# Attention layer of a four-layer GNN: rows kept turned, logits and coefficients laid out by edge in DRAM, products on GpSimd

## The reference

```python
h = relu(layernorm(x))
x1 = leaky(h, 0.01) @ W1.T + b1
h1 = (x1 @ Wg.T).reshape(N, 4, 32)
a_src = sum(h1 * att_src, axis=-1)
a_dst = sum(h1 * att_dst, axis=-1)
alpha = leaky(a_src[src] + a_dst[dst], 0.2)
coeff = softmax of alpha over the edges of one dst
out = segment_sum(h1[src] * coeff[:, :, None], dst)
out = leaky(out.reshape(N, 128) + bias_g, 0.01) @ W2.T + b2
x = x + out
```

## Time and profile before

| | |
|---|---|
| three runs | 3823.89, 3836.2 and 3827.94 us; median 3827.94 us |
| profiled execution, span | 3830.4 us (first to last instruction) |
| busy in the span | PE 1893.7, DVE 1993.0, ACT 992.0, POOL 2403.2 us |
| stage 3 | about 1281 to 1961 us |
| stage 4 | about 1961 to 2012 us |
| stage 5 | about 2012 to 2190 us |

### The profile page before, as it was taken

The page is one execution under the profiler, slowest core; times in us unless marked ns, Lnnn a source line. Parts: engine busy times, 40 slices in busy tenths (PEclk is TensorE's granted clock), DMA queues, the critical chain, the costliest instruction groups (busy, mean ns, idle before and its releaser), DMA issues. The chain is left out here.

```text
span 3830.4 us, 41092 instructions
## 1 busy us (share of the span) xinstructions
PE 1893.7 (49%) x8918; PEld 1513.8 (40%) x8918; DVE 1993.0 (52%) x6228; ACT 992.0 (26%) x2804; POOL 2403.2 (63%) x2088
## 2 busy tenths in 40 slices
PE   0000011158887467777655523247777773555553
PEld 0000010047676345555534412235555553545453
DVE  6964310058889534334458745543333334766664
ACT  0000010046561034334323334432222221221211
POOL 0867777768880455556500066548888886888887
PEclk9999985578899755555558855556666666776776
DMA  2999622246570122222207634446666664655555
GB/s 83 303 297 326 198 54 57 52 57 85 81 118 16 33 58 63 60 62 64 57 20 221 196 98 119 121 108 126 121 121 127 120 121 109 137 122 128 124 124 84
DMA packets 449554, 437.59 MB, mean 114 GB/s; under 512 B 77870, under 2 KB 359507, under 8 KB 449169
## 3 DMA queue, kind: packets, MB, share of 16 engines
q1 hardware_dynamic: 280404, 283.91, 23.7%
q0 software_dynamic: 128576, 119.75, 21.5%
q10 hardware_dynamic: 40512, 33.32, 3.7%
HBM read 262.12 MB, written 174.67 MB: 114 GB/s over the span
## 5 line engine op out<-in xcount | busy, mean ns | idle before, releaser
L1706 DVE TENSOR_TENSOR_SCAN work<-work,bank 128x512 f32<-128x512 f32 (+1 forms) x343 | 426.4, 1265 | 420.9 <-PE bank L842 272.2
L643 POOL DMA_INDIRECT work<-d,idx_run_d x196 | 191.2, 975 | 417.7 <-DVEq L286 294.7
L710 POOL DMA_INDIRECT big<-out_dram,idx_src_d x196 | 187.3, 956 | 308.7 <-DVE sc_d L1859 131.9
L657 POOL DMA_INDIRECT out_dram<-big,idx_add_s x196 | 310.0, 1582 | 83.5 <-issue 55.5
L657 POOL DMA_INDIRECT out_dram<-big,idx_add_d x196 | 314.0, 1602 | 77.2 <-issue 59.4
L657 POOL DMA_INDIRECT out_dram<-work,idx_add_s x196 | 315.9, 1612 | 70.9 <-issue 58.8
L1200 ACT ACTIVATE work<-work 128x128 f32<-128x128 f32 x784 | 318.3, 484 | 115.3 <-DVE work L1701 99.6
L842 PE MATMUL bank<-ident,work 128*128 128x128 f32 x588 | 143.8, 391 | 413.3 <-ACT work L1200 145.9
L842 PEld LDWEIGHTS bank<-ident,work 128*128 128x128 f32 x588 | 93.4, 195 | 456.1 <-issue 207.2
L643 POOL DMA_INDIRECT work<-rec_d,idx_e_s x196 | 216.7, 1106 | 80.6 <-issue 58.5
L643 POOL DMA_INDIRECT work<-he,idx_last_s x196 | 193.7, 988 | 87.2 <-issue 59.5
(11 more groups left out here) (340 smaller groups left out, 5508.1 us busy)
## 6 DMA issues: line engine op xcount, KB each, us to landing
out_dram<-big SPq DMA_DIRECT2D x71, 726.0 KB
big<-in_x_dram SPq DMA_DIRECT2D x71, 704.0 KB
work<-flags_src SPq DMA_DIRECT2D x98, 256.0 KB
work<-flags_dst SPq DMA_DIRECT2D x98, 256.0 KB
edge_w<-work SPq DMA_DIRECT2D x49, 512.0 KB
work<-edge_w ACTq DMA_DIRECT2D x49, 512.0 KB
gat_h<-work SPq DMA_DIRECT2D x49, 256.0 KB, 2.0
work<-gat_h SPq DMA_DIRECT2D x49, 256.0 KB, 4.2
```

What stands on the lines that cost most here:

```text
L643: g_.indirect_dma_start(to, None, table_ap, bass.IndirectOffsetOnAxis(ap=f[:, at_:at_ + 1], axis=0)).then_inc(of_rows(name).of(G), 16)
L657: g_.indirect_dma_start(table[:, :], bass.IndirectOffsetOnAxis(ap=of[:, at_:at_ + 1], axis=0), row, None, compute_op=ALU.add).then_inc(add ...
L710: g_.indirect_dma_start(to[:, t * ROW:(t + 1) * ROW], None, table, bass.IndirectOffsetOnAxis(ap=of[:, at_:at_ + 1], axis=0)).then_inc(rows ...
L1706: return V.tensor_tensor_scan(to, flag_r[G.place][rows, :], of, before if G.from_(1) else 0.0, ALU.mult, ALU.add)
```

## The change

Stage 3: PE projects the other way round, with the weights standing in the array and the turned rows streaming: one matmul of 512 columns for the rows and two of 512 columns for the logits of the four heads. The rows are stored turned (features by edges), and the bias is added by ACT in `keep`. The logits come out as 4 partitions of 512 edges, get their constant on DVE in one instruction, and go to DRAM (`gat_logits`). On ACT the copy of the turned rows (`rows_on`) is put one group later, ahead of `keep`.

Stage 4: the logits are loaded from DRAM in the softmax layout, the leaky step is done there, and the coefficients are stored to DRAM (`gat_coefficients`).

Stage 5: each group loads its coefficients as four transfers, one per head, each spread over 32 partitions; two are issued by SP and two by ACT. POOL multiplies rows by coefficients; there is no transpose; DVE scans the products from SBUF. The leaky step is one DVE instruction on the scan's result and on ACT's scaled copy.

```diff
+        def load_coefficients(eng, G, heads):
+            if G.from_(UNROLL):
+                eng.wait_ge(GATSUM["h"], G.g - (UNROLL - 1))
+            for h in heads:
...
+                eng.dma_start(co_r[G.place][C * h:C * h + C, :], part.partition_broadcast(C)).then_inc(h_in.of(G), 16)
...
@@ SP, stage 3 and stage 5
+            def store_logits(G):
+                sp.wait_ge(GAT["logits"], G.g + 1)
...
+                sp.dma_start(part, lg_r[G.slot][0:H, :]).then_inc(h_stored.of(G), 16)
...
                 sp.dma_start(in_r[G.place], at(h_dram, G, 512)).then_inc(h_in.of(G), 16)
+                load_coefficients(sp, G, (0, 1))
...
@@ POOL, stage 5
+            def products(G):
+                h_in.wait(pool, "GATSUM", G)
+                if G.from_(2):
+                    pool.wait_ge(GATSUM["chained"], G.g - 1)
+                g_.tensor_tensor(h_r[G.slot], in_r[G.place], co_r[G.place], ALU.mult).then_inc(GATSUM["h"], 1)
+            for_groups(pool, products)
...
@@ PE, stage 3
-                x_, b = hT8[G.slot], bank[4 + G.slot]
-                T.matmul(b[:, :], one[0:1, :], bF4[0:1, :], start=True, stop=False)
-                for t in range(GROUP):
-                    T.matmul(b[:, t * P:(t + 1) * P], x_[:, t * P:(t + 1) * P], wts["WF"][:, :],
-                             start=False, stop=t == GROUP - 1)
-                for t in range(GROUP):
-                    o = bank[6 + G.slot][:, t * H:(t + 1) * H]
-                    T.matmul(o, x_[:, t * P:(t + 1) * P], attF[:, 0:4], start=True, stop=False)
-                    last = T.matmul(o, x_[:, 512 + t * P:512 + (t + 1) * P], attF[:, 4:8], start=False, stop=True)
-                last.then_inc(GAT["hh"], 1)
+                x_ = hT8[G.slot]
+                T.matmul(bank[4 + G.slot][:, :], wts["WF"][:, :], x_[:, 0:512], start=True, stop=True)
+                o = bank[6 + G.slot][0:H, :]
+                T.matmul(o, attF[:, 0:H], x_[:, 0:512], start=True, stop=False)
+                T.matmul(o, attF[:, H:2 * H], x_[:, 512:1024], start=False, stop=True).then_inc(GAT["hh"], 1)
...
@@ ACT, stage 3
             def body(G):
                 deviations(G, GAT, W8)
...
                 norm(G, GAT, lambda t: v8[G.slot][:, t * P:(t + 1) * P], h8[G.slot], W8, small[G.slot])
+                if G.from_(1):
+                    if G.from_(3):
+                        act.wait_ge(GAT["hh"], G.g - 2)
+                    rows_on(G.before())
                 if G.from_(2):
                     keep(G.before(2))
-                act.wait_ge(GAT["hT"], G.g + 1)
-                for k in range(2):
-                    last = S_.copy(hT8[G.slot][:, k * 512:(k + 1) * 512], bank[2 * G.slot + k][:, :])
-                last.then_inc(GAT["hTs"], 1)
...
@@ ACT, stage 5
             def body(G):
-                if G.from_(1):
-                    biased(G.before())
-                if G.from_(2):
-                    keep(G.before(2))
+                load_coefficients(act, G, (2, 3))
+                if G.from_(2):
+                    biased(G.before(2))
+                if G.from_(3):
+                    keep(G.before(3))
...
@@ DVE, stage 5
+            def chain_products(G):
+                flags_at.wait(dve, "GATSUM", G)
+                dve.wait_ge(GATSUM["h"], G.g + 1)
...
+                run_scan(G, uT_r[G.slot], uT_r[1 - G.slot][:, 511:512], h_r[G.slot]).then_inc(GATSUM["chained"], 1)
...
-                done(V.scalar_tensor_tensor(z_r[G.slot], t1_r[G.slot], 0.01, t1_r[G.slot], ALU.mult, ALU.max))
-                need(order.off)
-                V.tensor_scalar(z_r[G.slot], z_r[G.slot], cols[:, 2:3], None, ALU.subtract).then_inc(GATSUM["z"], 1)
+                V.scalar_tensor_tensor(z_r[G.slot], uT_r[G.slot], cols[:, 5:6], t1_r[G.slot], ALU.add, ALU.max
+                                       ).then_inc(GATSUM["z"], 1)
...
             def body(G):
-                front(G)
-                if G.from_(2):
-                    leaky(G.before(2))
-                if G.from_(1):
-                    chain(G.before(), GATSUM, "GATSUM", [bank[1 - G.slot]], uT_r, "biased")
+                chain_products(G)
+                if G.from_(1):
+                    leaky(G.before())
```

More of the change, by code:

```diff
@@ L972, in delta @@
                 last.then_inc(GATSUM["delta"], 1)
[L974 to L980 removed]
+            for_groups(pe, delta)
             stage_end(pe, 5)
@@ L1251, in keep, with rows_on @@
                     h_stored.wait(act, "GAT", G.before(2))
-                S_.copy(hst_r[G.slot], bank[4 + G.slot][:, :]).then_inc(GAT["kept"], 1)
+                S_.activation(hst_r[G.slot], bank[4 + G.slot][:, :], ACT.Identity, bias=cols[:, 3:4]).then_inc(GAT["kept"], 1)
+            def rows_on(G):
+                act.wait_ge(GAT["hT"], G.g + 1)
+                for k in range(2):
+                    last = S_.copy(hT8[G.slot][:, k * 512:(k + 1) * 512], bank[2 * G.slot + k][:, :])
+                last.then_inc(GAT["hTs"], 1)
             def body(G):
```

113 lines of the change are left out of this document (44 added, 69 removed).

## The result

The changed kernel takes 3799.53 us (median of four runs, 3795.41 to 3805.58), the kernel before 3829.16 us (four runs, 3823.89 to 3836.2). The ratio is 0.9915 with a 95% interval of 0.9889 to 0.9941. It is faster, as forecast, but by 30 us where the forecast said 133: the time lies above the range of 3650 to 3785.

What follows compares the result with a forecast made beforehand. Late signals paced stage 3's loop at 12.99 us a group, and DVE's instructions filled most of stage 5. 3830.4 - 151 (stage 3) - 3 (stage 4) + 21 (stage 5) = 3697, as run median 3695 us; range 3650 to 3785.

Steps and rivals of the forecast that it cites:

- Stage 3, the term that decides: Stage 3: with three matmuls of 512 columns and the lateness gone, it ends 151 us earlier; bounds 0 and 162.
- the lateness of 7.5 us: Stage 3: every second projection is signalled 7.5 us late; taken to belong to the short matmuls and set to 0.4 us.
- The sign that the prediction named for being wrong: Stage 3: a `remote` wait of 7 us still ahead of the logits would show the forecast wrong.
- POOL becomes the bound: Stage 3: the loop falls to 9.1 us a group, less than POOL's 9.95, so POOL sets the pace.
- The estimate of the loop without lateness: Stage 3, new projection: 9.33 + 0.25 + 8.2 + 0.4 = 18.2 us for two groups, 9.1 a group.
- Stage 4: Stage 4: turns and copies go, a load and an uncovered store come in; 3 us less, between 6 less and 3 more.
- Stage 5: Stage 5: 3.8 us a group, 21 us more; bounds 3.2 (8 us less) and 4.4 (51 us more).
- the 0.2 that I added by choice: Stage 5: added to the largest of three close limits (3.2 to 3.6 us) sharing queues, giving 3.8 us a group.
- Taken one after the other: Stage 5: POOL's product, DVE's scan and leaky step do not overlap: 1.2 + 1.27 + 0.69 = 3.2 us a group.
- The DMA setup-cost knee: Stage 5: at 138 GB/s for 64 KiB transfers, four pieces cost 1.9 us, 4.6 us a group, 60 us more.
- The signal stays late every second group: Rival, stage 3: lateness stays, 12.7 us a group, gain 15 us at most; 3851 with stage 5 at 4.2; chance 0.10.
- Late once per pass of the loop: Rival, stage 3: late once every four groups, 11.0 us a group, 49 us more, kernel at 3744; chance 0.13.

Runs made afterwards that it cites:

- experiment 8: The kernel before, with SP loading side-by-side rows in stage 3 and no gathers by POOL: 3628.03 us (kernel before, there: 3834.22), stage 3 478.1 us.
- run 29: Not a label of a run: of the 44 signals sent later in such a run of gathers, 29 come over 1 us late.

## Why the prediction was wrong in size

**The step that failed** is in "Stage 3, the term that decides", where the lateness of 7.5 us is priced: "I take it to belong to the run of short matmuls, which goes, so I set it to 0.4 us". The changed kernel has no short matmuls, and its logits are late in 17 groups of 49 (86 us) and its root in 17 (92.5 us); experiment 8 has the short matmuls and no lateness. It belongs to unbroken runs of POOL's gathers. In the changed kernel a signal of DVE or PE that is sent in the first 10 us of a run, with a pause of 3 us or more ahead of the run, is at most 0.7 us late (34 of them); of the 44 sent later in such a run 29 come over 1 us late. (The 12 and 16 us that two expectations name hold in the kernel with fewer signals; here PE's signals are late from 10 us on.) The late signal holds DVE up, the ring fills, POOL pauses, and the next signals are prompt. In the kernel before this settled at 16 gathers and a pause of some 6 us. Its timeline has the same two projections as the earlier trace rows:

```profile
1855.74 0.94 POOL L710 DMA_INDIRECT big<-out_dram,idx_src_d  x1 [6.21 <-DVE sc_d L1859]
...
1856.14 0.57 PE L928 MATMUL bank<-attF,work 128*128 128x4 f32 x2
...
1870.60 0.57 PE L928 MATMUL bank<-attF,work 128*128 128x4 f32 x2
...
1874.77 0.95 POOL L710 DMA_INDIRECT work<-out_dram,idx_dst_d  x1 [0.30 <-issue]
```

One signal falls 1 us into the run and is prompt; the next falls 15 us into it and is 7.5 us late, at 1878.63. That regular beat looked like a property of the code. In the changed kernel a first run of 56 gathers is followed by runs of 8 to 32, with pauses of 1.3 to 9 us. The sign that the prediction named for being wrong, a `remote` wait ahead of the logits, is there (75.6 us).

**"POOL becomes the bound"** therefore did not come true: a POOL that never pauses is the very state in which signals are late. The forecast had POOL at 9.95 us a group. The changed kernel has 12.2 on average ((1882.5 - 1283.1) / 49), and with breaks POOL is the bound, at 11.9.

**The estimate of the loop without lateness** came near for the projection before: 18.4 us for two groups, some 450 to 490 us for the stage; measured without gathers, 478.1. Part of that is luck, as PE's own work of 446 us is the bound there and not the loop. For the new one it was too long (9.1 us a group; measured 7.9), as I priced matmuls of 512 columns at 2.07 us, the row of the lower clock; at the clock that the stage was granted most of them take 1.02.

**Stage 4** gained 0.6 us for a forecast of 3, inside its bounds. From the coefficients' store (1968.10) to the next stage's first load (1971.16) there are 3.06 us, priced at 2.4.

**Stage 5** came out as forecast in kind and nearly in size: 13 us more for 21. Groups and two rows of the timeline in the changed kernel:

```profile
L742 POOL TENSOR_TENSOR work<-work 128x512 f32<-128x512 f32 x49 | 67.1, 1369 | 204.9 <-DMA work<-gat_coefficients 202.1 <-DVE work L1716 2.7
L1716 DVE TENSOR_TENSOR_SCAN work<-work 128x512 f32<-128x512 f32 x49 | 62.8, 1282 | 92.9 <-POOL work L742 91.3 <-ACT work L1297 1.2 <-DVE work L1925 0.4
```

```profile
L742 POOL TENSOR_TENSOR work<-work x49: 1255/1271/1775, 1978.3 to 2153.2; 128x512 f32<-128x512 f32 x49
```

```profile
1983.72 1.26 POOL L742 TENSOR_TENSOR work<-work 128x512 f32<-128x512 f32 x1 [1.18 <-DMA work<-gat_coefficients]
1983.84 1.70 DVE L1925 SCALAR_TENSOR_TENSOR work<-work,cols 128x512 f32<-128x512 f32 x1
```

The product recurs every 3.64 us ((2153.2 - 1978.3) / 48); transfers had been put at 3.6 and ACT's loads at 3.6, and the 0.2 that I added by choice is the excess. The row of L742 names what ends last: the coefficients' landing, 202.1 us. The product takes 1.27 us (priced 1.2) where it runs alone. The scan waits for it, so the two hardly ever run together (0.4 us in the whole stage), and the scan's 1.28 us tell nothing of POOL. The leaky step does run beside the product, and there the pair of the earlier trace rows recurs: in the two cases where the product started first, by 0.12 and 0.14 us, the step took 1.70 and 1.69 us in place of 0.72 and ended after the product; where the step started first, the product took up to 1.77. Taken one after the other, as the prediction had it, they still fit beside the transfers. The loads of 64 KB land after a median of 4.2 us on ACT's queue and 4.4 on SP's. By the estimate that the prediction worked out from the Trainium skill, SBUF — State Buffer, "The DMA setup-cost knee", the stage would have grown by 60 us; this trace does not bear that out: its transfers keep a share of 0.90 at 261 GB/s and the stage grew by 13.

**The rivals.** "The signal stays late every second group" named the right thing, but put the sum at 3851 by way of a stage 5 of 4.2 us a group and a fixed 7.5 us; its gain of at most 15 us in stage 3 was 41. The root and the logits were late in about a third of the groups each. (By its own figures, 49 x (25.98 - 25.3) / 2, that gain is 17 us and not 15.) "Late once per pass of the loop" gave 3744. The 17 late roots fall 5, 5, 4 and 3 times on the four places of a pass, and without gathers the loops of DVE, ACT and PE, unchanged, have no late signal; so the rule behind that rival (the Trainium skill, Runtime: NRT & Kernel Launch, "Instruction fetch mechanics") is not what acts here. The evidence for the first rival stood in the rows and was stated: the other projection of each pair has the same short matmuls and is on time. I gave it 0.10 against a guess that no row showed. What the same timeline could have told is that what differs between the two projections is how long POOL had been gathering.

**The range** took its low and high ends from cases in which the lateness goes or becomes rarer by a fixed amount; a feedback that shortens and lengthens it was in none of them.

## What to carry to other kernels

Where a wait is long and its releaser had long ended, ask what else runs at that moment, and mark each late signal on the timeline of the other engines before its cause is put on the producer. A run of gathers that POOL issues without a break is such a neighbour: try a wait for its own rows after each group, which costs one line and here gained more than the rewritten projection did. And before a stage is forecast to be bound by another engine, ask whether that engine's full pace leaves the rest as prompt as it was.

## What the runs showed of the hardware

- While POOL issues indirect gathers back to back, signals of DVE and of PE that are sent more than 10 us into such a run, or behind a pause of under 2 us, reach the waiting engines up to 8.95 and 13.4 us late in the changed kernel; ACT's signals to PE do not (at most 0.14 us in 49 of 49). In the three kernels without gathers none of 441 roots, logits and transposes is more than 0.16 us late.
- Beside the gathers DVE's instructions are held up also where they neither wait nor signal: 194 of 1176 added clearings of 59 ns, 146 us in all, in steps of 0.7 us. With those clearings it began 3 us into a run (behind a pause of 6.1 us), so the length of the run is not the only condition.
- Breaks of 1.8 to 1.9 us after each 10 us of gathers keep the root's and the logits' signals prompt (two kernels, 0 of 98 late in each); while POOL gathers, these are all sent in the first 6 us of a run there. Breaks of 1.1 us after each 10 us, or of 1.8 after each 20, do not (31 and 33 of 98 late).
- The number of DVE's signals, the arrivals and bytes of SP's loads, the inputs of DVE's subtractions and buffers between DVE and ACT make no difference to it. Why gathers hold up DVE's instructions and PE's signals, and not ACT's, stays open. Every run here was recorded, instruction by instruction. Whether the recording has a part in the steps of 0.7 us can't be told, as no run is without it.
- A DVE step with two inputs in SBUF that starts 0.12 to 0.14 us after a product of POOL takes 1.70 us in place of 0.72 and ends after the product (2 of 49).
- The granted clock of stage 3 went from 0.50 to 0.69 when 34 matmul records a group (1666 in 49) became 14 (686), and to 0.78 with those and no gathers; with the old projection and no gathers, PE busy 446 of 478 us, it stayed at 0.50. That of stage 5 fell from 0.84 to 0.51 when its transposes went; the stage waits for transfers there, so it cost nothing that these runs show.
